# Local attention in a one-core kernel: each tile's values projected once and spread over partitions by DMA, a new order on TensorE, and the feed-forward part in blocks of 512 tokens

## What is computed

```python
DIM, DEPTH, HEADS, DIM_HEAD, WINDOW = 128, 6, 16, 64, 32   # INNER = 1024, DIM_INNER = 341

def local_attention(q, k, v):          # windows of 32 tokens; a window sees itself and the one before
    ...
    bk2, bv2 = look(bk), look(bv)
    mask = (it < jb) | (it > jb + w) | (jb == -1)
    sim = jnp.einsum('bhwie,bhwje->bhwij', bq, bk2) * QK_SCALE
    attn = jax.nn.softmax(jnp.where(mask, -big, sim), -1)
    return jnp.einsum('bhwij,bhwje->bhwie', attn, bv2)

def attn_layer(x, Wqkv, qs, ksc, Wo):
    q, k, v = heads of jnp.split(x @ Wqkv, 3, -1)
    q, k = rotary(l2norm(q) * qs), rotary_inverse_scale(l2norm(k) * ksc)
    return local_attention(q, k, v) @ Wo

def ffn_layer(x, g, bln, W1, b1, W2, b2):   # x: half of the features shifted by one token
    xn = layernorm(x) * g + bln
    a, gate = jnp.split(xn @ W1 + b1, 2, -1)
    return a * gelu(gate) @ W2 + b2
...
for r in range(DEPTH):
    x = x + attn_layer(x, ...)
    x = x + ffn_layer(shift_tokens(x), ...)
```

## Time and profile before

| | us |
|---|---|
| median of three runs | 3558.05 (3556.76 to 3558.65) |
| the profiled execution, its own time | 3553.56 |
| its span, from the first to the last instruction | 3551.6 |
| TensorE busy in the span | 3145.7 (89%) |
| VectorE / ScalarE / GpSimd busy | 2420.1 (68%) / 1954.6 (55%) / 1288.0 (36%) |
| part that the change touches, first scores to the end of the last visit | 1665.7 to about 3507 |

### The profile page before, as it was taken

The page is one execution under the profiler, slowest core; times in us unless marked ns, Lnnn a source line. Parts: engine busy times, 40 slices in busy tenths (PEclk is TensorE's granted clock), DMA queues, the critical chain, the costliest instruction groups (busy, mean ns, idle before and its releaser), DMA issues.

```text
span 3551.6 us, 74661 instructions
## 1 busy us (share of the span) xinstructions
PE 3145.7 (89%) x30196; PEld 1853.3 (52%) x30196; DVE 2420.1 (68%) x3958; ACT 1954.6 (55%) x5084; POOL 1288.0 (36%) x851
## 2 busy tenths in 40 slices
PE   4669676749797999995999999999999999999997
PEld 3534464523344233333666666666666666666664
DVE  4940397359803877775877777777777777777774
ACT  3222410254222466664777777677777767777773
POOL 0010001000000111113666666656666665666662
PEclk7579855879899899998999999999999999999999
DMA  2000000000000100002000000000000000000000
GB/s 95 3 0 0 34 3 2 1 0 0 0 0 29 47 22 24 21 18 85 2 2 13 2 32 2 13 2 32 13 2 32 2 14 1 32 2 2 2 1 13
DMA packets 16501, 53.38 MB, mean 15 GB/s; under 512 B 4064, under 2 KB 6368, under 8 KB 14272
## 3 DMA queue, kind: packets, MB, share of 16 engines
q1 hardware_dynamic: 16192, 49.02, 4.0%
HBM read 43.57 MB, written 5.44 MB: 14 GB/s over the span
## 4 chain that ended last, share of the span: by engine, by line
PE 77%; DVE 15%; DVEq 2%; issue 2%; ACT 2%; DMA 1%; POOLq 1%; ACTq 0%; POOL 0%; SPq 0%
PE ps L1475 19%; PE ps L648 6%; PE ps L1527 5%; PE ps L1517 5%; PE ps L1535 5%; PE ps L1493 5%; PE ps L1508 4%; DVE arena L972 4%; PE ps L1076 4%; PE ps L1548 4%; PE ps L1104 4%; PE ps L1091 3%; PE ps L1553 2%; PE ps L1500 2%; PE ps L200 1%
## 5 line engine op out<-in xcount | busy, mean ns | idle before, releaser
L1475 PE MATMUL ps<-arena 128*128 128x512 f32 (+1 forms) x1536 | 742.7, 606 | 16.2 <-ACTq L1790 14.5
L1864 ACT ACTIVATE arena<-ps,arena 128x96 f32<-128x96 f32 x1536 | 497.7, 349 | 165.7 <-DVE arena L2071 165.5
L2151 POOL TENSOR_TENSOR arena<-arena 128x1024 f32<-128x1024 f32 x190 | 447.6, 2361 | 221.3 <-DVE arena L1945 221.3
L2157 POOL TENSOR_TENSOR arena<-arena 128x2048 f32<-128x2048 f32 x95 | 344.2, 3623 | 259.3 <-ACT arena L1797 252.9
L1241 DVE TENSOR_REDUCE arena<-ps 128x1 f32<-128x512 f32 x512 | 329.4, 686 | 77.1 <-PE ps L1076 72.0
L1475 PEld LDWEIGHTS ps<-arena 128*128 128x128 f32 (+1 forms) x1536 | 244.8, 177 | 233.9 <-issue 214.5
L1203 ACT ACTIVATE arena<-ps 128x1024 f32<-128x1024 f32 x256 | 262.2, 1024 | 178.5 <-PE ps L1091 178.0
L2146 POOL TENSOR_TENSOR arena<-arena 128x768 f32<-128x768 f32 x192 | 282.7, 1472 | 135.7 <-DVE arena L1979 135.7
L1864 ACT ACTIVATION_READ_ACCUMULATOR arena<-ps,arena 128x1 f32 x1536 | 330.7, 215 | 0.0
L1940 DVE TENSOR_TENSOR arena<-ps,arena 128x1024 f32<-128x1024 f32 x192 | 234.2, 1220 | 67.0 <-PE ps L1475 46.9
L191 POOL TENSOR_SCALAR rstd<-mv 128x4 f32<-128x4 f32 x32 | 8.1, 254 | 717.5 <-DVE mv L178 717.5
(11 more groups left out here) (289 smaller groups left out, 5605.9 us busy)
## 6 DMA issues: line engine op xcount, KB each, us to landing
arena<-in_deep SPq DMA_DIRECT2D x6, 2649.5 KB, 9.6
arena<-in_rotary SPq DMA_DIRECT2D x6, 1024.0 KB, 4.8
pack_tern<-in_tern SPq DMA_DIRECT2D x2, 2888.0 KB, 10.5
arena<-scr_q SPq DMA_DIRECT2D x96, 48.0 KB
arena<-scr_k SPq DMA_DIRECT2D x96, 48.0 KB
scr_q<-arena SPq DMA_DIRECT2D x10, 256.0 KB, 3.0
arena<-in_mod SPq DMA_DIRECT2D x1, 1536.0 KB, 6.6
scr_k<-arena SPq DMA_DIRECT2D x6, 256.0 KB, 3.4
```

The costliest lines, as they stand in the source:

```text
L1475: last = T.matmul(m.ps[0:rows.stop - rows.start, at + half, :], f.xs[t % 2][:, rows], w.wqkv[:, j * INNER + half * BLK:j * INNER + (half + ...
L1864: last = A(f.prob[:, p, :], m.ps[:, 4 + j % 2, i * SPAN:(i + 1) * SPAN], ACT.Exp, bias=f.nmax[t % 2][:, p:p + 1], accum_out=f.rsum[t % 2][ ...
L2151: G.tensor_tensor(f.rot[t % 2][:, here], f.rot[t % 2][:, here], f.sin[:, here], ALU.add)
L2157: G.tensor_tensor(r, r, spread(f.ss[t % 2], DH), ALU.mult).then_inc(s["rotated"], 1)
```

## The change

- **Values.** `values(t, at)` projects the 128 tokens of a tile once, in one pair of matmuls (128 stationary columns), at the end of the visit before. VectorE copies the result to a buffer `f.vraw` (`copy_values`); ScalarE's copy goes. SyncE's queue then moves pieces of it by DMA to the layout that `heads` reads (`spread_values`): 64 partitions to the first half's rows 32 to 95, 96 partitions to the second half's, and the last 32 partitions to the first 32 rows of the next tile's buffer. The last of these waits until `heads` of the tile two before has read that buffer. `heads` waits for the moves (`v_spread`) in place of the copies.
- **Order on TensorE.** `scores(t, 2)` stands directly after `heads`, ahead of `keys`, except in visits with Gelus, where it stands behind the feed-forward matmuls. The first pair of value matmuls between `scores(t, 2)` and `outputs` is gone.
- **VectorE and ScalarE.** VectorE rotates the keys directly when they are made, and ScalarE squares the keys after VectorE, behind the last exponentials (in visits with Gelus ahead of them). `copy_values` also waits for the moves of the tile before.
- **Feed-forward part by blocks.** A block n of 512 tokens (4 tiles) starts when its four tiles are done, and one block's 11 matmuls are spread over visits with t % 4 = 1, 2, 3, 0, 1, 2, 3: `centre`; `variance`; one gate; two gates; two of the value side and the Gelus; the third; `second`. So from visit 8 on every visit carries feed-forward work: two matmuls for t % 4 = 0, three for 1, two for 2, four for 3. All go through banks 2 and 3 (one through 7) in place of 6 and 7, and so behind `q_squared`. After the last visit the rest of block 22 (eight matmuls, two of them before `end`) and block 23 are left.
- **Buffers and queue.** Six temporary tiles instead of ten; SyncE issues the weights and rotary tables of later rounds between the moves.

The diff, cut to its core:

```diff
-    def values(t, half, at):
-        project(t, at, 2, slice(HALF * half, HALF * half + SPAN)).then_inc(s["v_made"], 1)
+    def values(t, at):
+        project(t, at, 2, slice(WIN, KEYS)).then_inc(s["v_made"], 1)
...
+    def ffn(t):
+        q, r = divmod(t, 4)
+        if r == 0 and q >= 2:
+            first(q - 2, 1, 1, 2)
+            first(q - 2, 2, 1, 3)
+        elif r == 1 and q >= 1:
+            pe.wait_ge(s["shifted"], q)
+            centre(q - 1, 2)
+            if q >= 2:
+                first(q - 2, 0, 0, 3)
+        elif r == 2 and q >= 1:
+            pe.wait_ge(s["c_read"], 2 * q)
+            variance(q - 1, 2)
+            if q >= 2:
+                first(q - 2, 2, 0, 3)
+        elif r == 3 and q >= 1:
+            if q >= 2:
+                pe.wait_ge(s["glu"], 3 * (q - 2) + 3)
+                second(q - 2, 2)
+            pe.wait_ge(s["hn"], q)
+            first(q - 1, 0, 1, 3)
...
     def visit(t):
+        gelu = t % 4 == 1 and t > 8
...
         if behind:
-            pe.wait_ge(s["v_copied"], 2 * t)
+            pe.wait_ge(s["v_spread"][(t - 1) % 2], 16 * v_moves(t - 1))
             pe.wait_ge(s["p_copied"], 2 * t)
             heads(t - 1)
+        if not gelu:
+            pe.wait_ge(s["exped"], 4 * t + 2)
+            scores(t, 2)
         if ahead2:
...
             keys(t + 2)
-        if h > 0 and 1 <= c <= 6:
-            pe.wait_ge(s["o_copied"], t)
-            ffn_pair(h - 1, c)
-        pe.wait_ge(s["exped"], 4 * t + 2)
-        scores(t, 2)
-        if ahead1:
-            if ahead2:
-                pe.wait_ge(s["q_squared"], t + 3)
-            else:
-                pe.wait_ge(s["v_copied"], 2 * t + 2)
-            values(t + 1, 0, V0_AT)
+            pe.wait_ge(s["q_squared"], t + 3)
+        else:
+            pe.wait_ge(s["v_copied"], t + 1)
+        ffn(t)
+        if gelu:
+            pe.wait_ge(s["exped"], 4 * t + 2)
+            scores(t, 2)
+        ffn_third(t)
         if behind:
-            if h > 0 and 1 <= c <= 6:
-                ffn_one(h - 1, c)
             pe.wait_ge(s["o_copied"], t)
             outputs(t - 1)
...
# ScalarE
+    def ffn_early(t):
+        q, r = divmod(t, 4)
+        if r == 1 and q >= 2:
+            gelus(q - 2)
             act.preload_act_table_set(EXP_LN)
...
         if ahead2:
             act.wait_ge(s["sumsq"], t + 2)
             square_queries(t + 2)
-            square_keys(t + 2)
+            if gelu:
+                square_keys(t + 2)
...
         exponentials(2)
         exponentials(3)
+        if ahead2 and not gelu:
+            square_keys(t + 2)
...
# SyncE
+    def spread_values(t):
+        raw, v = f.vraw[t % 2], f.v
+        sp.wait_ge(s["v_copied"], t + 1)
+        sp.dma_start(v[t % 2][WIN:SPAN, 0, :], raw[0:HALF, :]).then_inc(s["v_spread"][t % 2], 16)
+        sp.dma_start(v[t % 2][0:SPAN, 1, :], raw[WIN:P, :]).then_inc(s["v_spread"][t % 2], 16)
+        if t % BT != BT - 1:
+            if t >= 1:
+                sp.wait_ge(s["heads"], t)
+            sp.dma_start(v[(t + 1) % 2][0:WIN, 0, :], raw[P - WIN:P, :]).then_inc(s["v_spread"][(t + 1) % 2], 16)
```

More of the change, by code:

```diff
@@ L1465, in deep_at, with v_moves @@
     return h, c, rnd, b
+def v_moves(t):
+    return sum(2 + (u % BT != 0) for u in range(t % 2, t + 1, 2))
 def deep_tensor(nc, pe, m, s, f):
@@ L1536, in outputs, with centre @@
         last.then_inc(s["y"], 1)
[L1539 to L1546, removed]
+    def centre(n, bank):
+        T.matmul(m.ps[:, bank, :], f.centre, f.xc[n % 2], start=True, stop=True).then_inc(s["filled"], 1)
@@ L1547, in first, with variance @@
+    def variance(n, bank):
+        T.matmul(m.ps[:, bank, :], f.mean, f.dev, start=True, stop=True).then_inc(s["filled"], 1)
+    def first(n, k, gate, bank):
+        w, rows = f.w[n // 4 % 2], FF_ROWS[k]
         at = gate * FF + k * P
-        T.matmul(m.ps[0:rows, bank, :], w.w1[:, at:at + rows], f.xc[i], start=True, stop=True).then_inc(s["filled"], 1)
-    def second(e, i, bank):
-        w = f.w[e // BATCH % 2]
+        T.matmul(m.ps[0:rows, bank, :], w.w1[:, at:at + rows], f.xc[n % 2], start=True, stop=True)\
+            .then_inc(s["filled"], 1)
@@ L1552, in second @@
+    def second(n, bank):
+        w = f.w[n // 4 % 2]
         for k, rows in enumerate(FF_ROWS):
-            last = T.matmul(m.ps[:, bank, :], w.w2[0:rows, k, :], f.gl[3 * i + k][0:rows, :], start=k == 0, stop=k == 2)
+            last = T.matmul(m.ps[:, bank, :], w.w2[0:rows, k, :], f.gl[k][0:rows, :], start=k == 0, stop=k == 2)
         last.then_inc(s["filled"], 1)
[L1556 to L1578, removed]
@@ L1754, in deep_tensor @@
         visit(t)
-    end(VISITS - 1)
-    last_ffn(HALVES - 1)
+    n = BLOCKS - 1
+    pe.wait_ge(s["added"], n - 1)
+    first(n - 1, 1, 1, 2)
+    pe.wait_ge(s["g_copied"], 3 * (n - 1) + 1)
+    first(n - 1, 2, 1, 3)
+    end(VISITS - 1)
+    pe.wait_ge(s["shifted"], n + 1)
+    centre(n, 4)
+    first(n - 1, 0, 0, 5)
+    pe.wait_ge(s["g_copied"], 3 * n)
+    first(n - 1, 1, 0, 2)
+    pe.wait_ge(s["added_y"], VISITS)
+    final(0, 6)
+    pe.wait_ge(s["c_read"], 2 * n + 2)
+    variance(n, 3)
+    first(n - 1, 2, 0, 0)
+    pe.wait_ge(s["glu"], 3 * n)
+    second(n - 1, 1)
+    pe.wait_ge(s["hn"], n + 1)
+    first(n, 0, 1, 7)
+    first(n, 1, 1, 4)
+    first(n, 2, 1, 5)
+    pe.wait_ge(s["added"], n)
+    final(1, 1)
+    first(n, 0, 0, 2)
+    pe.wait_ge(s["rstd"], 2 * n + 1)
+    first(n, 1, 0, 3)
+    first(n, 2, 0, 0)
+    pe.wait_ge(s["glu"], 3 * n + 1)
+    final(2, 6)
+    pe.wait_ge(s["glu"], 3 * n + 3)
+    second(n, 7)
+    pe.wait_ge(s["added"], n + 1)
+    final(3, 1)
 def deep_scalar(nc, act, m, s, f):
@@ L2064, in visit @@
     def visit(t):
-        h, c, rnd, b = deep_at(t)
         behind, ahead2, ahead1 = t > 0, t + 2 < VISITS, t + 1 < VISITS
-        late = h > 0 and c in (4, 5)
+        gelu = t % 4 == 1 and t > 8
         def maxima(j):
@@ L2239, in deep_sync @@
     weights(1)
-    for rnd in range(2, DEPTH):
-        sp.wait_ge(s["products"], 2 * BATCH * BT * (rnd - 1))
-        rotary(rnd % 2)
-        sp.wait_ge(s["added"], 4 * (rnd - 1))
-        weights(rnd)
+    for t in range(VISITS):
+        spread_values(t)
+        h, c, rnd, b = deep_at(t)
+        if b == 1 and c == BT - 1 and rnd + 2 < DEPTH:
+            rotary(rnd % 2)
+        if b == 0 and c == BT - 1 and 0 < rnd and rnd + 1 < DEPTH:
+            sp.wait_ge(s["added"], 4 * rnd)
+            weights(rnd + 1)
     sp.wait_ge(s["rotary"], 16 * DEPTH)
```

437 lines of the change are left out of this document (179 added, 258 removed).

## The result

The changed kernel takes 3433.69 us, the median of four runs (3430.09 to 3436.24), against 3557.41 us for the kernel before in the same comparison: a ratio of 0.9653, 95% interval 0.964 to 0.9665. The forecast was 3440 us.

The account below looks back on a forecast made before the run. TensorE was taken to bound the kernel: 3553.6 - 166 + 3 + 52 + 1 - 7 = 3436 us for the profiled execution, 3440 us for the median of runs, with a range of 3385 to 3500 us.

Parts of the forecast that it names:

- What bounds: Stretch the change touches: TensorE sets the pace, busy 1831.5 of 1844 us, so time taken from it counts in full.
- the removed pair: Value matmuls on TensorE: 95 pairs gone at 1.75 us each, -166 us.
- The wait in visits with Gelus: TensorE waits 1.55 us for squared queries and 0.8 us ahead of the turn, in 22 visits: +52 us.
- The other visits: Visits without Gelus: 0.2 us wait for exponentials in five visits without feed-forward work, +1 us, none elsewhere.
- the second rival: Another chain, VectorE's above all, binds in most visits: 3473 to 3519 us; 21 in 100.
- The third: Rival: waits in Gelu visits lower TensorE's granted clock, 35 us lost, 3475 us; 4 in 100.
- The moves: DMAs of values from SBUF to SBUF: 3 to 5 us each, hidden; bound 9.6 us, hidden as well.
- The rival's "about 3590": Moves come late and heads waits: slower, about 3590 us if a move lands at 17 us; 5 in 100.
- Start and end: First pair, ahead of the visits, saves nothing; last visit +2 us and less work behind it -9 us, together -7 us.
- "TensorE waits anyway": Start, ahead of the visits: TensorE waits there anyway, so the first removed pair was not counted.

Follow-up runs that it names:

- pair_twice: The changed kernel with the pair of value matmuls issued twice in each visit, order and moves kept: 3594.46 us.
- order_alone: The kernel before, both value pairs kept, with scores and VectorE's maxima ahead of the keys outside visits with Gelus: 3566.65 us.
- scores_first: The changed kernel with the second part of the scores ahead of the wait for squared queries and the feed-forward matmuls in Gelu visits: 3393.94 us.
- no_gelu: The changed kernel with each Gelu replaced by a copy of one column, TensorE's order kept: 3396.85 us.
- late_scores: The changed kernel with the order of the Gelu visits in all visits from 1 on: 3586.48 us.
- best: scores_first with the order of before at the start, ScalarE squaring keys of tiles 0 and 1 before VectorE rotates them: 3391.4 us.
- late_filled: late_scores with one more pair of projections, its result unread, behind the outputs in visits 1 to 3: 3584.62 us in a single run.

## Why the prediction was right

**What bounds** the kernel and the removed pair: right. pair_twice costs 161 us where 163 were expected. In the change itself it brought more: a visit with two feed-forward matmuls takes 16.89 us, less 1.72 for these 15.17, against 17.01. That is 1.84 us a visit, above the bounds of 1.72 to 1.79: 95 x 1.84 = 175 us for 166. The 0.1 us beyond the pair's own 1.72 is about what the new order gains in order_alone where it costs nothing else; the prediction had no term for it.

**The wait in visits with Gelus**: right in place, releasers and nearly in size: 1.34 and 0.69 us as idle time (from start to start the first is the 1.5 forecast), and 20.34 us for the visit where 20.1 were forecast. By the visit's length (20.34 less 15.17 and three matmuls, 2.57) it is 2.6 us, times 22, 57 us for 52. scores_first and no_gelu remove it from its two sides.

**The other visits**: 15.45, 16.9 and 18.6 us, as forecast (15.3 to 15.6, 17.0, 18.7), except visit 2 with 15.74, where TensorE waits 0.37 us for the last exponentials ahead of the turn. TensorE waits for no step of VectorE's in visits 1 to 93, so the second rival is out. The third is out too: the granted clock of the Gelu visit is 1.00, and its turns take 1.94 us. That these visits have room rests on the new order: late_scores, which gives up the place of the scores and of the keys' steps together, loses 153 us, of which the sum that I made from rows had 115.

**The moves**: right; 2.3 to 4.1 us, hidden; 4.6 us more for the last one changed nothing. The rival's "about 3590" for moves that land at 17 us was wrong by its own figures (from 1.25 us of waiting at 16 us, one more in 95 visits gives some 3650), but nothing hangs on it.

**Start and end**: mis-sized. "TensorE waits anyway" at the start left out that the chain of VectorE and ScalarE sets it: +3.5 us, which best takes back. With the new order of squares VectorE's sums wait for the keys' squares, and the first turn comes 1.2 us later; the rest, 2.3 us, comes where ScalarE squares queries and keys of tile 1, each behind VectorE's products, ahead of the copies (L1785, L1787) that the first scores need. At the end the stretch from the last attention output to the output's DMA takes 23.3 us for 35.9, 12.6 less, where 9 were taken and 12 were the bound; from visit 95's scores to that attention output it takes 1.1 us more, where 2 were taken. The remaining 3.1 us ahead of the part are within the scatter from one execution to the next: in the profiles of the eight kernels with the changed last part, whose code ahead of it is the same, the first table's DMA starts anywhere from 1628.6 to 1634.2 us.

Together: -175 + 57 + 3 and 1 for the visits, less 3.4 of visit 95's matmuls that the measured stretch doesn't hold, and +1.7 for the longer waits of visit 0 (17.26 us, 2.09 above 15.17; before 17.39, 0.38 above 17.01): -115, against -114.9 measured; then +3.5, -11.5 and +3.1.

The mechanism was right, and the closeness is in part luck. For the profiled execution 3436 us were forecast and 3433.74 measured, because the misses cancel: the pair brought 9 us more and the end, with visit 95's matmuls counted there, 8 more, while the Gelu visits, visit 0, the start and the scatter ahead of it took 14 back. Of the 6 us between 3440 and the median of 3433.69, 4.5 are the distance between profiled execution and median, which the kernel before had and the changed one hasn't.

## What to carry to other kernels

Where an engine has no idle time over a long stretch, work taken from it counts at its start-to-start price (here 1.72 us a pair), but only if the chain that was hidden behind that work is shortened with it: here the last exponentials would have been late, and the scores had to move ahead of the keys and the keys' squares behind the exponentials. When work moves into a buffer that another engine empties, look what else stands behind that wait in an in-order queue: putting the scores ahead of it, a move of a few lines, was worth 40 us more. A copy that only rearranges partitions can go to DMA if its reader comes a whole visit later, as here, where the last move lands 12 us ahead of its reader.

## What the runs showed of the hardware

After 3.11 us without a matmul the granted clock of TensorE was 0.53 in the following 3.6 us, mostly its lower level of 1.2 GHz, and 16 turns took 3.60 us; after 1.39 us they took 1.94. So an idle time of 3.1 us cost 4.8 in visit 1 of late_scores (and 5.9 in visit 4 of late_filled), and a filler of 1.7 us in it made the visit 1.7 us shorter. Between these, after 2.25 us, the clock fell in two visits of late_scores and not in a third. The Trainium skill ("TensorE: Matmul & The Clock Gate", What's actually happening) says that activity releases the throttle; by that rule the trace agrees. I had weighed this for the change, where waits in the visits with Gelus are short enough (1.34 and 0.69 us); in late_scores I did not, and it is most of that kernel's miss in the first visits. A DMA from SBUF to SBUF on SyncE's queue took 2.3, 3.5 and 4.1 us from issue to landing for 128, 256 and 384 KB on 32, 64 and 96 partitions; the two larger were in flight together, so that their times alone are not known. The prediction's estimate of 2.3 to 2.9 us fits the smallest and is short for the others. It rests on the Trainium skill ("DMA: Bandwidth & Descriptors", Anatomy of one DMA), which gives its figures for DMAs issued from GpSimd.
